# A three-stage transformer layer on one core: the gate chain kept in a PSUM bank, accumulators copied ahead of the bands, the query-key banks copied in another order, the context transposed earlier

## What is computed

```
x = x + attention(layernorm(x))         # one score matrix per sequence, scores times a factor set by
                                        # bands of sigmoid(score), softmax, values, projection
x = x + xattn(layernorm(x), ctx, ctx)   # 8 heads of 32; itilde and ftilde are linear in q, k, v
    csum   = cumsum(log_sigmoid(ftilde))
    Dtilde = csum_i - csum_j + itilde_j   (j <= i);  max_d = max over j
    C      = (q k^T) * exp(Dtilde - max_d) / sqrt(32)
    H      = C v / (max(|sum C|, exp(-max_d)) + 1e-6), then a norm per head
x = x + ffn(layernorm(x))               # 256 -> 1024 -> 256, exact gelu, low-rank terms from tokens 1 to 16
```

## Time and profile before

| what | value |
|---|---|
| median of 3 runs | 1925.06 us |
| the profiled execution, its own time | 1924.64 us |
| its span | 1922.9 us |
| TensorE busy | 1809.3 us (94%) |
| VectorE busy | 1571.9 us (82%) |
| ScalarE busy | 1081.1 us (56%) |
| GpSimd busy | 335.0 us (17%) |
| TensorE in 56.80 us, one looped step (900.00 to 956.80) | 55.27 us busy, granted clock 1.00 |
| chain that ended last | PE 77%, DVE 10%, issue 7%, ACT 5% |
| share of VectorE's L965 in that chain | 3% |

### The profile page before, as it was taken

The page is one execution under the profiler, slowest core; times in us unless marked ns, Lnnn a source line. Parts: engine busy times, 40 slices in busy tenths (PEclk is TensorE's granted clock), DMA queues, the critical chain, the costliest instruction groups (busy, mean ns, idle before and its releaser), DMA issues.

```text
span 1922.9 us, 44190 instructions
## 1 busy us (share of the span) xinstructions
PE 1809.3 (94%) x14040; PEld 1362.2 (71%) x14040; DVE 1571.9 (82%) x4524; ACT 1081.1 (56%) x2440; POOL 335.0 (17%) x269
## 2 busy tenths in 40 slices
PE   5589999999999999999999999999999999999988
PEld 4457777777777777777777777777777777777766
DVE  6687888898888888888889888888888888888752
ACT  1355566555566655556655556665556665555552
POOL 2121121122022112112112102211211211210210
PEclk9789999999999999999999999999999999999999
DMA  4101111111111111111111111111111111111100
GB/s 119 31 28 26 35 45 47 39 42 25 44 36 47 47 36 46 25 35 45 47 38 44 24 42 39 47 47 36 46 25 35 45 47 37 45 24 39 32 15 25
DMA packets 205743, 75.57 MB, mean 39 GB/s; under 512 B 150273, under 2 KB 205186, under 8 KB 205714
## 3 DMA queue, kind: packets, MB, share of 16 engines
q1 hardware_dynamic: 205714, 75.21, 15.1%
HBM read 53.93 MB, written 16.78 MB: 37 GB/s over the span
## 4 chain that ended last, share of the span: by engine, by line
PE 77%; DVE 10%; issue 7%; ACT 5%; DMA 0%; SPq 0%; DVEq 0%; ACTq 0%
PE UA L1376 17%; PE UB L1376 5%; PE TB L1453 3%; PE GT L1386 3%; DVE bands L965 3%; PE TA L1343 3%; PE TA L1453 3%; PE UB L1318 3%; PE TA L1283 3%; PE TA L1184 3%; PE TB L1184 3%; PE UA L1318 3%; ACT QKs L694 3%; PE PV L1318 2%; PE UB L1420 2%
## 5 line engine op out<-in xcount | busy, mean ns | idle before, releaser
L1376 PE MATMUL UA<-W2f,hs_all 128*128 128x256 f32 x1536 | 350.8, 381 | 3.8 <-DVE ot L1022 3.1
L1376 PEld LDWEIGHTS UA<-W2f,hs_all 128*128 128x128 f32 x1536 | 286.5, 190 | 67.0 <-ACT hs_all L704 14.1
L1039 DVE TENSOR_TENSOR C<-qT,QKs 128x512 f32<-128x512 f32 x256 | 166.2, 690 | 113.7 <-ACT qT L713 104.4
L598 POOL TENSOR_TENSOR Ng<-HT,gnw_b 128x256 f32<-128x256 f32 x128 | 105.4, 824 | 823.2 <-ACT HT L726 823.2
L579 POOL TENSOR_TENSOR xg<-x,gnb_b 128x1024 f32<-128x1024 f32 x32 | 83.9, 2621 | 682.6 <-ACT ot L668 645.6
L1376 PE MATMUL UB<-W2f,hs_all 128*128 128x256 f32 x512 | 115.8, 379 | 0.0
L612 ACT ACTIVATE lv<-ve 128x4 f32<-128x4 f32 x95 | 19.1, 202 | 164.2 <-DVE ve L831 164.2
L694 ACT ACTIVATE QKs<-TA 128x512 f32<-128x512 f32 x64 | 38.4, 600 | 125.3 <-PE DD L1343 125.3
L1376 PEld LDWEIGHTS UB<-W2f,hs_all 128*128 128x128 f32 x512 | 95.0, 190 | 11.7
L1343 PEld LDWEIGHTS TA<-xn2T,ctxT 32*128 32x128 f32 x512 | 63.3, 190 | 43.6 <-issue 41.1
L1343 PE MATMUL TA<-xn2T,ctxT 32*128 32x128 f32 x512 | 74.9, 286 | 19.3 <-DVE acs L969 17.1
(11 more groups left out here) (328 smaller groups left out, 5146.2 us busy)
## 6 DMA issues: line engine op xcount, KB each, us to landing
...
bands<-ctx SPq DMA_DIRECT2D x256, 64.0 KB, 1.9
...
Ev<-xn SPq DMA_DIRECT2D x512, 1.0 KB
...
E<-xn SPq DMA_DIRECT2D x128, 16.0 KB
T<-tok SPq DMA_DIRECT2D x128, 8.0 KB, 1.7
```

Source lines behind the costliest of these rows:

```text
L598: pool.tensor_tensor(Ng[:, b, :].rearrange("p (k n) -> p k n", k=2), HT[:, b % 2, :, 0:P], gnw_b[:, :].rearrange("p (k n) -> p k n", k=2), ...
L1039: dve.tensor_tensor(C[:, b % 2, :, half], dx[hf].rearrange("p (h i) -> p h i", h=HEADS), QKs[:, b, :, half], ALU.mult)\
L1376: ins = pe.matmul(OB[b][:, 0:D], hs_all[:, k, b * S:(b + 1) * S], W2f[:, k, :], start=(i == 0), stop=(i == KH - 1))
```

## The change

- gabs and lsig are no longer SBUF tiles but columns 128 to 383 of bank GT; ScalarE writes and reads them there, and VectorE's two operations read lsig and gabs from it.
- VectorE's copy of the accumulators into acs and all that leads to rows stand ahead of the first two band comparisons. sums() writes its two products in exchanged columns; the running maximum goes from the copy and from DD straight into a third part of acs, acs_ok comes after it, and the tile am and its copy are gone.
- keep_qk copies DD, QQ, TA, GT. decay(0, 0) waits for the fifth copy, decay(0, 1) for the sixth.
- The context's blocks have a tile of their own. SyncE loads them behind T, when the transpose of the step before is done. VectorE transposes them behind the first norm's statistics, ahead of C(0, 0).
- The context for the values is loaded straight into vc, behind E, when the last pv of the step is done; GpSimd takes the differences in place and then writes the ones with one more operation, which waits for them.
- VectorE's C(1, 0) and C(1, 1) stand ahead of ln_scale(0).

```diff
-        ctx_blocks = bands[:, :, :].rearrange("p k (n c) -> p k n c", c=32)
-        ctxn = sb("ctxn", [P, G, D])
+        blocks = sb("blocks", [P, 2, N])
+        ctx_blocks = blocks[:, :, :].rearrange("p k (n c) -> p k n c", c=32)
-        gabs = sb("gabs", [P, P])
-        lsig = sb("lsig", [P, P])
-        acs = sb("acs", [32, 2 * P])
-        am = sb("am", [32, 2, P])
+        acs = sb("acs", [32, 3, P])
+        gabs, lsig = GT[:, P:2 * P], GT[:, 2 * P:3 * P]
...
                 if FFN.on(it):
                     t_rows(it)
+                if SELF.on(it):
+                    sp.wait_ge(ctxT_ok.h, ctxT_ok.at(it, 0))
+                    for h in range(HEADS):
+                        sp.dma_start(ctx_blocks[32 * (h % 4):32 * (h % 4) + 32, h // 4, :, :],
+                                     c_blocks[it][:, :, 32 * h:32 * h + 32]).then_inc(blocks_loaded.h, 16)
                 if COMING.on(it):
                     sp.wait_ge(xb_ok.h, xb_ok.at(it, 1))
                     sp.dma_start(xin[:, :, :], x_g[it + 1]).then_inc(x_loaded.h, 16)
-                if SELF.on(it):
-                    sp.wait_ge(vc_ok.h, vc_ok.at(it, 1))
-                    sp.dma_start(ctxn[:, :, :], c_g[it]).then_inc(ctx_loaded.h, 16)
...
                 if CROSS.on(it):
                     e_rows(it)
+                if SELF.on(it):
+                    sp.wait_ge(pv_mm.h, pv_mm.at(it, G))
+                    sp.dma_start(vc[:, :, :], c_g[it]).then_inc(ctx_loaded.h, 16)
...
                     pool.wait_ge(ctx_loaded.h, ctx_loaded.at(it, 0))
-                    pool.wait_ge(pv_mm.h, pv_mm.at(it, 0))
...
+                    pool.wait_ge(diff_ok.h, diff_ok.at(it, 1))
+                    last = heads[:, :, HD - 1:HD]
+                    ones = one[:, 0:1].unsqueeze(1).broadcast_to([P, G * HEADS, 1])
+                    pool.tensor_tensor(last, ones, ones, ALU.mult).then_inc(vc_ok.h, 1)
...
-                    for r in range(4):
+                    for r in (3, 1, 0, 2):
...
-                if own:
-                    dve.wait_ge(sc_ok.h, sc_ok.at(it, 1))
-                    band_lo = v.mark(dve.tensor_scalar(band_a[:, :], sc[:, :], BANDS[0], 0.3, ALU.is_ge, ALU.mult))
-                    band_hi = v.mark(dve.tensor_scalar(band_b[:, :], sc[:, :], BANDS[3], None, ALU.is_gt))
                 if cross:
                     dve.wait_ge(sel_mm.h, sel_mm.at(it, 1))
-                    dve.tensor_copy(acs[:, :], DD[0:32, 0:2 * P]).then_inc(acs_ok.h, 1)
+                    link(dve.tensor_copy(acs[:, 0:2, :].rearrange("p a n -> p (a n)"), DD[0:32, 0:2 * P]))
+                    dve.tensor_tensor_scan(acs[:, 2, :], acs[:, 1, :], DD[0:32, P:2 * P], -3e38,
+                                           ALU.max, ALU.max).then_inc(acs_ok.h, 1)
                     dve.wait_ge(acs_ok.h, acs_ok.at(it, 1))
-                    run_max = v.mark(dve.tensor_tensor_scan(am[:, 1, :], acs[:, 0:P], acs[:, 0:P], -3e38,
-                                                            ALU.max, ALU.max))
-                    dve.tensor_copy(am[:, 0, :], acs[:, 0:P])
...
+                if own:
+                    dve.wait_ge(blocks_loaded.h, blocks_loaded.at(it, HEADS * 16))
+                    dve.wait_ge(qk_mm.h, qk_mm.at(it, 2))
+                    dve.transpose(ctxT[:, :, :].rearrange("p k n -> p (k n)"),
+                                  blocks[:, :, :].rearrange("p k n -> p (k n)")).then_inc(ctxT_ok.h, 1)
                 if cross:
                     weigh_qk(0, 0)
                     weigh_qk(0, 1)
                 if ffn:
                     gT_copy()
+                if cross:
+                    weigh_qk(1, 0)
+                    weigh_qk(1, 1)
                 if coming:
                     dve.wait_ge(rs0_ok[0].h, rs0_ok[0].at(it, 1))
                     ln_scale(0, link)
                 if cross:
-                    weigh_qk(1, 0)
-                    weigh_qk(1, 1)
...
-                    pe.matmul(DD[0:32, 0:P], sel_i[:, :], csum[:, :], start=True, stop=True)
-                    pe.matmul(DD[0:32, P:2 * P], sel_f[:, :], csum[:, :], start=True, stop=True).then_inc(sel_mm.h, 1)
+                    pe.matmul(DD[0:32, P:2 * P], sel_i[:, :], csum[:, :], start=True, stop=True)
+                    pe.matmul(DD[0:32, 0:P], sel_f[:, :], csum[:, :], start=True, stop=True).then_inc(sel_mm.h, 1)
...
+                    if k < 2:
+                        pe.wait_ge(QKs_ok.h, QKs_ok.at(it, 5 + k))
                     if k == 0:
-                        pe.wait_ge(QKs_ok.h, QKs_ok.at(it, 8))
```

More of the change, by code:

```diff
@@ L187, in build @@
         cut = sb("cut", [P, 1])
+        one = sb("one", [P, 1])
         lntau = sb("lntau", [P, 1])
@@ L395, in build @@
         xb_ok = per_step("xb_ok", SELF, 1)
+        diff_ok = per_step("diff_ok", CROSS, 1)
         vc_ok = per_step("vc_ok", CROSS, 1)
@@ L548, in _ @@
                                pattern=[[-HD, 4]], channel_multiplier=1)
-            pool.memset(vc[:, :, HD - 1::HD], 1.0)
+            pool.memset(one[:, :], 1.0)
             pool.memset(lntau[:, :], LN_TAU)
@@ L670, in step @@
                     act.wait_ge(gate_ok.h, gate_ok.at(it, 1))
-                    a.link(act, act.activation(gabs[:, :], gate[:, :], ACT.Abs))
-                    a.link(act, act.activation(lsig[:, :], gabs[:, :], ACT.Exp, scale=-1.0, bias=cut[:, 0:1]))
-                    act.activation(gabs[:, :], lsig[:, :], ACT.Ln, bias=1.0).then_inc(lnsig_ok.h, 1)
+                    a.link(act, act.activation(gabs, gate[:, :], ACT.Abs))
+                    a.link(act, act.activation(lsig, gabs, ACT.Exp, scale=-1.0, bias=cut[:, 0:1]))
+                    act.activation(gabs, lsig, ACT.Ln, bias=1.0).then_inc(lnsig_ok.h, 1)
                 if SELF.on(it):
@@ L958, in step @@
                     dve.wait_ge(lnsig_ok.h, lnsig_ok.at(it, 1))
[L959 to L960 removed]
+                    link(dve.scalar_tensor_tensor(lsig, gate[:, :], cap[:, 0:1], gabs, ALU.min, ALU.subtract))
+                    dve.tensor_tensor_scan(csum[:, :], carry[:, :], lsig, 0.0, ALU.mult, ALU.add)\
                        .then_inc(csum_ok.h, 1)
[L963 to L966 removed]
                 if cross:
                     dve.wait_ge(sel_mm.h, sel_mm.at(it, 1))
[L969 removed]
+                    link(dve.tensor_copy(acs[:, 0:2, :].rearrange("p a n -> p (a n)"), DD[0:32, 0:2 * P]))
+                    dve.tensor_tensor_scan(acs[:, 2, :], acs[:, 1, :], DD[0:32, P:2 * P], -3e38,
+                                           ALU.max, ALU.max).then_inc(acs_ok.h, 1)
                     dve.wait_ge(acs_ok.h, acs_ok.at(it, 1))
[L971 to L974 removed]
                     dve.wait_ge(em_mm.h, em_mm.at(it, 0))
[L976 to L977 removed]
+                    arg = v.mark(dve.tensor_tensor(em[0:32, :], acs[:, 2, :], acs[:, 0, :], ALU.add))
+                    neg = v.mark(dve.tensor_scalar(acs[:, 2, :], acs[:, 2, :], -1.0, None, ALU.mult))
                     dve.wait_ge(v.h, v.upto(arg))
@@ L981, in step @@
                     dve.wait_ge(v.h, v.upto(neg))
-                    link(dve.tensor_copy(parts[0:32, :, :], am[:, :, :]))
-                    link(dve.tensor_tensor(amr[:, :, :], am[:, :, :], parts[0:32, :, :], ALU.subtract))
+                    link(dve.tensor_copy(parts[0:32, :, :], acs[:, 1:3, :]))
+                    link(dve.tensor_tensor(amr[:, :, :], acs[:, 1:3, :], parts[0:32, :, :], ALU.subtract))
                     link(dve.tensor_copy(am2[:, :, :], amr[:, :, :]))
@@ L994, in step @@
                 if own:
+                    dve.wait_ge(sc_ok.h, sc_ok.at(it, 1))
+                    band_lo = v.mark(dve.tensor_scalar(band_a[:, :], sc[:, :], BANDS[0], 0.3, ALU.is_ge, ALU.mult))
+                    band_hi = v.mark(dve.tensor_scalar(band_b[:, :], sc[:, :], BANDS[3], None, ALU.is_gt))
                     dve.wait_ge(v.h, v.upto(band_lo))
@@ L1092, in step @@
                 if own:
-                    dve.wait_ge(blocks_loaded.h, blocks_loaded.at(it, HEADS * 16))
-                    dve.wait_ge(qk_mm.h, qk_mm.at(it, 2))
-                    dve.transpose(ctxT[:, :, :].rearrange("p k n -> p (k n)"),
-                                  bands[:, :, :].rearrange("p k n -> p (k n)")).then_inc(ctxT_ok.h, 1)
                     dve.wait_ge(probs_ok.h, probs_ok.at(it, 1))
```

17 lines of the change are left out of this document (3 added, 14 removed).

## The result

| what | before | after |
|---|---|---|
| median | 1924.64 us (4 runs, 1922.93 to 1925.23) | 1895.96 us (4 runs, 1895.52 to 1896.05) |
| ratio | | 0.9852, 95% interval 0.9835 to 0.9869 |
| span of the profiled execution | 1922.9 us | 1894.2 us |
| one looped step, from up(0) to the next up(0) | 56.82 us (926.83 to 983.65) | 55.87 us (913.08 to 968.95) |
| TensorE busy | 94% | 96% |

The forecast was 1891.2 us with a range of 1882 to 1916. The kernel became 28.7 us faster (1924.64 - 1895.96), where 33.9 were forecast. (56.82 - 55.87) x 30 steps = 28.5 us, so the looped steps hold nearly all of it.

A forecast was written before the change was run, and what follows sets the result against it. TensorE was taken as the bound, busy 94%, waiting mainly for acs before qk(0) and before pv(1). 30 x (0.69 + 0.44) = 33.9 us gave 1891.2 us, range 1882 to 1916.

The forecast's parts named there:

- Gate chain and copy order: Adapter to qk(0): scan freed, copy acs ahead of the bands, so qk(0) no longer waits; 0.69 us a step.
- the gain hangs on the copy's place ahead of the bands, and the bank adds little: Before qk(0): were the scan still held until 934.43, only 0.06 of the 0.69 us would be lost.
- QKs order: ScalarE's QKs copies: decay products can start sooner, but down(0) still needs the fifth Gelu; 0 us.
- ln_scale held: VectorE after C(1,1): one of ln_scale(0)'s four small steps waits 0.45 us for GpSimd's first Ng.
- pv(2) set by C(2,1): Second value products: C(2,1) ends near 957.14, pv(2) starts near 957.24 against 957.38, leaving 0.14 us.
- pv(3), 0.44: Transpose no longer ahead of C(3,1): pv(3) at 960.21 instead of 960.65, 0.44 us a step.
- today's 3.27 less 0.30 of waiting: Spacing from pv(2) to pv(3) without the wait for C(3,1), forecast as 2.97 us.
- B: Rival: GpSimd's second Ng comes ahead of C(2,1), making pv(3) 0.35 us later than before; 1914.9 us, chance 0.16.
- C: Rival: the bank doesn't free the scan; 1.07 us a step gained, 1893.0 us, chance 0.06.
- D: Rival: ln_scale isn't held, pv(3) at 960.06; 1.28 us a step gained, 1886.7 us, chance 0.06.
- E: Rival, slower: two waits behind GpSimd's Ng operations put pv(3) 1.05 us later than before; 1935.9 us, chance 0.04.
- From there to the next adapter TensorE's own order holds: From pv(3) to the next adapter: VectorE and ScalarE have over 2 us of room before xn2 and xn3.

The follow-up runs named there:

- transpose_late: The changed kernel with the transpose of the context blocks back behind head_sums(1), ahead of C(3,0): 1930.85 us, ratio 1.0038.
- no_bank: The changed kernel with the gate chain back in SBUF tiles, the copy acs still ahead of the bands: 1897.26 us, ratio 0.9857.
- one_last_pt: The kernel one_last with ScalarE's copy PT between HT and the square behind it instead of after the square: 1886.97 us, ratio 0.9808.
- ln_scale_last: The changed kernel with ln_scale(0) behind C(3,1) instead of ahead of head_sums(0): 1921.22 us, ratio 0.9982.
- one_last: The changed kernel with the 32-byte tile one at the end instead of ahead of other tiles: 1890.55 us, ratio 0.9826.

## Why the prediction was right, and where it was wrong

**Gate chain and copy order, 0.69 us a step: right.** Adapter to up(5) takes 3.98 us instead of 4.68, 0.70 less, and the rest of the chain is as the text had it: scan 0.42, the ones 0.31 (taken as 0.3), no wait for acs. The addition into em ended at 922.02 + 0.32 = 922.34, 2.30 us after the adapter; held to 936.0, as the text had it, is 2.31. That the ends agree is partly luck: it was hardly held at all (0.32 us for 0.27 before), it came late because the copy did. The trace agrees with the Trainium skill, SBUF — State Buffer, section Who interferes with whom, now for a scan as well: with one of its two inputs in PSUM it takes 0.42 us beneath GpSimd's second operation (transpose_late), with both in SBUF 2.64 (no_bank). The sentence "the gain hangs on the copy's place ahead of the bands, and the bank adds little" is what the two kernels show: without the bank the median is 1.3 us higher, within the spread of the runs, without the order 21.7. Even with the bands first the bank adds nothing.

**QKs order, 0: right**, by the rows (1.28 and 1.27 us); not tried on its own.

**ln_scale held, 0.45: right**, 0.43 (0.60 instead of 0.17), by the Ng that was named. The one that was held is the third (L840), which has one tensor input; the text had looked at the three with two. pv(1) gained 0.36, not 0.29: the text took 0.19 us from the end of an Exp to its product from rows in which VectorE was busy until 955.07 (954.66 + 0.41) anyway. In the changed kernel the Exp ends at 938.47 and C(1,1) starts at 938.51.

**pv(2) set by C(2,1): wrong.** The size was near (0.23 gained from down(0) to pv(2), forecast 0.14), the reason was not. C(2,1) ended at 942.52 and pv(2) started at 942.88. I had followed VectorE alone and not asked what else stood between pv(1) and pv(2) on TensorE: mix(0) needs PT, and once pv(1) came earlier, PT was 0.13 us late. one_last_pt shows that PT was the limit, ln_scale_last that C(2,1) was not.

**pv(3), 0.44: the size right by luck**, 0.43. It came as 0.23 at pv(2) and 0.20 behind it, where 0.14 and 0.30 were forecast: two misses that cancel. The step that failed is "today's 3.27 less 0.30 of waiting". No row shows 0.30; in every kernel in which pv(3) doesn't wait for C it comes 3.07 us behind pv(2), so the wait was 0.20. What the forecast had right is the reason: the wait for C(3,1) went with the transpose. The transpose cost nothing where it now stands, as forecast: VectorE still idles 2.09 us behind it.

**Rivals.** B (the second Ng ahead of C(2,1)) didn't come about: C(2,1) was under way when the Ng started at 942.39. C and D fall by the scan and by the held step. E's mechanism didn't occur; the side that it stood for is real, though: transpose_late, a small variation of this very kernel, is slower than the kernel before, by a meeting that no rival named.

**The step that failed in the sum** is one that isn't in it: "From there to the next adapter TensorE's own order holds" took TensorE's products to last as long as before. Those of up() didn't: 0.18 us a step, 5.4 us in all, with the 32 bytes of the tile one. Without them the forecast would have been met: one_last, which is the change with that tile at the end, measured 1890.55 us, and 1891.2 was forecast. That hit owes its closeness to the luck named at pv(3).
